# Last phase of a two-layer metaformer: two of eight normalisations and a bias move from ACT and DVE to POOL, and DVE adds the residual a slot later

## The reference, cut to what matters

```python
y = conv(dw3(dw2(dw1(x))), pw_w)          # 1x1 convolution after three depthwise ones
x = x + y * x_normed                      # gate
t = tokens(x)                             # [pixels, 96]
n = (t - mean(t)) / sqrt(var(t) + 1e-5)   # over the 96 channels
h = relu(q16(q16(q8(n) @ W1.T) + q8(b1)))
t = t + q16(q16(q8(h) @ W2.T) + q8(b2))
```

## Time and profile before

| | us |
|---|---|
| median of 3 runs | 3661.55 (3657.33 to 3664.26) |
| the profiled execution's own time | 3659.49 |
| its span | 3657.6 |
| phase C | from about 2500 to the end |

### The profile page before, as it was taken

One profiled execution on the slowest core, in us unless ns is written; L12 is line 12 of the kernel. 1 busy time (PEld: TensorE's weight loads), 2 busy tenths in 40 slices (PEclk: granted clock), 3 DMA queues, 4 the chain that ended last, 5 costly groups with the idle time before them and its releaser, 6 DMA issues. The chain is left out here.

```text
span 3657.6 us, 68122 instructions
## 1 busy us (share of the span) xinstructions
PE 3017.4 (82%) x21990; PEld 1910.0 (52%) x21990; DVE 3218.4 (88%) x8131; ACT 2781.3 (76%) x6274; POOL 1728.9 (47%) x2404
## 2 busy tenths in 40 slices
PE   6787888878787878887876799997888888888887
PEld 5565665656565656565654344443444444444444
DVE  4888889898989898989886699999899999999998
ACT  2577777777777877777778455554799999999998
POOL 3777777777787877787864000000222222222221
PEclk9999999899999999999987899999999999999999
DMA  3233323232323232323212888897676667666762
GB/s 68 53 89 74 91 71 88 71 88 70 88 71 88 71 88 71 88 71 88 71 56 69 212 238 234 236 280 212 172 199 188 181 185 200 184 184 193 199 177 83
DMA packets 696178, 478.92 MB, mean 131 GB/s; under 512 B 407217, under 2 KB 674422, under 8 KB 683830
## 3 DMA queue, kind: packets, MB, share of 16 engines
q1 hardware_dynamic: 695830, 474.58, 49.2%
HBM read 272.09 MB, written 201.92 MB: 130 GB/s over the span
## 5 line engine op out<-in xcount | busy, mean ns | idle before, releaser
L1891 POOL TENSOR_SCALAR C_var<-C_st 128x16 f32<-128x16 f32 x64 | 13.5, 211 | 1338.6 <-DVE C_st L178 1338.6
L1464 DVE SCALAR_TENSOR_TENSOR B_y<-B_mid,B_coefs,B_y 128x512 f32<-128x512 f32 x768 | 509.0, 750 | 3.2 <-ACT B_y L1429 3.2
L1395 PE MATMUL B_ps_row<-B_z,B_band 128*128 128x512 f32 x1152 | 499.1, 596 | 15.1 <-DMA B_band<-edge_scratch 15.1
L378 DVE TENSOR_SCALAR A_hq<-A_h,A_b 128x512 f16<-128x512 f16 x768 | 319.4, 456 | 176.5 <-ACT A_h L370 169.6
L370 ACT ACTIVATE A_h<-A_hid 128x512 f16<-128x512 f32 x768 | 428.3, 594 | 59.5 <-PE A_hid L357 57.1
L178 DVE BATCH_NORM_STATS2 A_st<-A_xT 128x6 f32<-128x192 f32 x1536 | 443.6, 349 | 29.3 <-ACT A_xT L861 16.0
L370 ACT ACTIVATE C_h<-C_hid 128x512 f16<-128x512 f32 x768 | 425.0, 589 | 22.9 <-PE C_hid L357 22.5
L1504 ACT ACTIVATE C_q<-C_xT,C_shift,C_rstd 128x96 fp8e5<-128x96 f32 x1024 | 392.6, 457 | 43.3 <-POOL C_shift L1898 43.2
L894 ACT ACTIVATE A_xc<-A_xT,A_shift,A_rstd 128x96 f32<-128x96 f32 x1024 | 379.3, 456 | 4.2 <-POOL A_shift L1207 4.0
L167 POOL TENSOR_TENSOR A_rstd<-A_var,A_expo 128x16 f32<-128x16 f32 x128 | 376.5, 2941 | 10.7
L1395 PEld LDWEIGHTS B_ps_row<-B_z,B_band 128*128 128x128 f32 x1152 | 218.8, 190 | 294.2 <-issue 287.8
(11 more groups left out here) (167 smaller groups left out, 7248.7 us busy)
## 6 DMA issues: line engine op xcount, KB each, us to landing
A_xq<-in_x SPq DMA_DIRECT2D x32, 1536.0 KB, 8.9
x_scratch<-A_xT SPq DMA_DIRECT2D x64, 768.0 KB, 3.2
x_scratch<-A_x3h SPq DMA_DIRECT2D x64, 768.0 KB, 5.4
B_z<-x_scratch SPq DMA_DIRECT2D x96, 512.0 KB
y_scratch<-B_y SPq DMA_DIRECT2D x96, 512.0 KB, 3.6
C_x3q<-x_scratch SPq DMA_DIRECT2D x32, 1536.0 KB, 9.1
C_xT<-x_scratch SPq DMA_DIRECT2D x64, 768.0 KB, 16.6
C_y3q<-y_scratch SPq DMA_DIRECT2D x31, 1536.0 KB, 15.6
```

Source lines behind the costliest of these rows:

```text
L378: r = dve.tensor_scalar(self.hq[:, b, s], self.h16[:, b, s], self.w["b1"][:, j:j + 1], 0.0, ALU.add, ALU.max)
L1395: m = pe.matmul(bank(c, h), band[c.buf(NB)][:, d, :], z[c.buf(NB)][:, half(h), d:d + W], start=(d == 0), stop=(d == 2))
L1464: dve.scalar_tensor_tensor(y, mid[c.buf(2)][:, half(h), t:t + W], coefs[:, c.n, 3 + t:4 + t], y, ALU.mult, ALU.add).then_inc(ev["sums"], 1)
```

## The change

- `LN_AT` loses groups 3 (slot 0) and 7 (slot 4). POOL normalises them in `pool_norm`, with two tensor operations per group: scale by the reciprocal deviation into a new float32 tile `scaled`, then add the shift into `q8`. New semaphores `normp` and `scaled` go with it. POOL does group 7 of a unit in its slot 1 and group 3 of the next unit in slot 5.
- `dve_y` becomes `pool_y`: the second layer's bias is added by POOL, for all 8 groups, in slots 1 to 8.
- DVE's `out` of group k moves from the end of slot k+1 to slot k+2, and there it stands behind `dve_hidden` and in front of `gate`. `out` of group 7 goes to slot 0 of the next step.

```diff
-LN_AT = {6: (1, 0), 7: (1, 1), 8: (1, 2), 0: (0, 3), 1: (0, 4), 2: (0, 5), 3: (0, 6), 4: (0, 7)}
+LN_AT = {6: (1, 0), 7: (1, 1), 8: (1, 2), 1: (0, 4), 2: (0, 5), 3: (0, 6)}
+POOL_GROUP = 3
...
+    def pool_norm(self, pool, i, k):
+        ev, t = self.ev, slice(k * TPC, (k + 1) * TPC)
+
+        pool.wait_ge(ev["ln2"], ev.at("ln2", i, k // 4))
...
+        x = self.x_of(i)[:, k * CW:(k + 1) * CW].rearrange("p (t c) -> p t c", c=C)
+        pool.tensor_tensor(self.scaled[:], x, per_token(self.rstd[:, t], TPC), ALU.mult).then_inc(ev["scaled"], 1)
+        pool.wait_ge(ev["scaled"], ev.at("scaled", i, k // 4))
+        pool.tensor_tensor(self.q8[:, t, :], self.scaled[:], per_token(self.shift[:, t], TPC), ALU.add,
+                           saturate=False).then_inc(ev["normp"], 1)
...
-    def dve_y(self, dve, i, k):
+    def pool_y(self, pool, i, k):
         ev = self.ev
 
-        dve.wait_ge(ev["y16"], ev.at("y16", i, k))
-        dve.tensor_scalar(self.y16b[:, k % 2, :], self.y16[:, k % 2, :], self.w["b2"][:, 0:1], None,
-                          ALU.add).then_inc(ev["yb"], 1)
+        pool.wait_ge(ev["y16"], ev.at("y16", i, k))
+
+        if k >= 2:
+            pool.wait_ge(ev["out"], ev.at("out", i, k - 2))
...
+        pool.tensor_scalar(self.y16b[:, k % 2, :], self.y16[:, k % 2, :], self.w["b2"][:, 0:1], None,
+                           ALU.add).then_inc(ev["yb"], 1)
...
             def body(i):
-                q = i + 1
+                q, p = i + 1, i - 1
                 for s in range(FFN_SLOTS):
                     if i.real and s < NK:
                         ff.dve_hidden(dve, i, s)
+                    if s == 0 and p.real:
+                        out(p, NK - 1)
+                    if i.real and s >= 2:
+                        out(i, s - 2)
                     if q.real and s < NK:
                         gate(q, s)
                     if q.real and s >= 1:
                         x4(q, s - 1)
-                    if i.real and s >= 1:
-                        ff.dve_y(dve, i, s - 1)
                     if q.real and s >= 1:
                         stats(q, s - 1)
-                    if i.real and s >= 1:
-                        out(i, s - 1)
...
             def body(i):
                 q = i + 1
-                for half in range(2):
-                    if q.real:
-                        norm_terms(q, half)
+                for s in range(1, FFN_SLOTS):
+                    if i.real:
+                        ff.pool_y(pool, i, s - 1)
+                    if i.real and s == 1:
+                        ff.pool_norm(pool, i, 4 + POOL_GROUP)
+                    if q.real and s % 4 == 0:
+                        norm_terms(q, s // 4 - 1)
+                    if q.real and s == 5:
+                        ff.pool_norm(pool, q, POOL_GROUP)
```

More of the change, by code:

```diff
@@ L1494, in __init__, with normed @@
         self.shift = sb("shift2", [P, NT], F32)
+        self.scaled = sb("scaled", [P, TPC, C], F32)
+    def normed(self, i, k):
+        if k % 4 == POOL_GROUP:
+            return self.ev["normp"], self.ev.at("normp", i, k // 4)
+        return self.ev["norm2"], self.ev.at("norm2", i, k - k // 4)
+    def pool_norm(self, pool, i, k):
+        ev, t = self.ev, slice(k * TPC, (k + 1) * TPC)
+        pool.wait_ge(ev["ln2"], ev.at("ln2", i, k // 4))
+        earlier = i if k // 4 else i - 1
+        if begun(earlier):
+            pool.wait_ge(ev["normp"], ev.at("normp", earlier, 1 - k // 4))
+        if begun(i - 1):
+            pool.wait_ge(ev["q8_full"], ev.at("q8_full", i - 1, k))
+        x = self.x_of(i)[:, k * CW:(k + 1) * CW].rearrange("p (t c) -> p t c", c=C)
[3 more added lines that the diff above has]
+                           saturate=False).then_inc(ev["normp"], 1)
     def act_norm(self, act, i, k):
@@ L1509, in pe_q8 @@
         ev, ring = self.ev, self.ring
-        pe.wait_ge(ev["norm2"], ev.at("norm2", i, k))
+        pe.wait_ge(*self.normed(i, k))
         name, unit, pos = ring.before(step, "q8", k)
@@ L1546, in act_y @@
         act.activation(self.y16[:, k % 2, :], self.ring.bank("y", k)[0:C, 0:CH], ACT.Copy).then_inc(ev["y16"], 1)
-    def dve_y(self, dve, i, k):
+    def pool_y(self, pool, i, k):
         ev = self.ev
-        dve.wait_ge(ev["y16"], ev.at("y16", i, k))
-        dve.tensor_scalar(self.y16b[:, k % 2, :], self.y16[:, k % 2, :], self.w["b2"][:, 0:1], None,
-                          ALU.add).then_inc(ev["yb"], 1)
+        pool.wait_ge(ev["y16"], ev.at("y16", i, k))
+        if k >= 2:
+            pool.wait_ge(ev["out"], ev.at("out", i, k - 2))
+        elif begun(i - 1):
+            pool.wait_ge(ev["out"], ev.at("out", i - 1, NK - 2 + k))
+        pool.tensor_scalar(self.y16b[:, k % 2, :], self.y16[:, k % 2, :], self.w["b2"][:, 0:1], None,
+                           ALU.add).then_inc(ev["yb"], 1)
 class LastBuffers:
@@ L1632, in phase_c @@
                 back_uses += [("y", s - 1, 0, "y16", s - 1), ("c", s - 1, 0, "out", s - 1)]
-        ev = Events(nc, ctx, "C_", dict(x1=NK, bn2=NK, ln2=2, ln2_s=6, norm2=NK, q8_full=NK, y_full=NK, c_full=NK, q8c=NK,
+        ev = Events(nc, ctx, "C_", dict(x1=NK, bn2=NK, ln2=2, ln2_s=6, norm2=NK - 2, normp=2, scaled=2, q8_full=NK, y_full=NK, c_full=NK, q8c=NK,
                                         hidden=NJ * NK, h16=NJ * NK, relu=NK, hq=NK, y16=NK, yb=NK, out=NK, pw_full=NK,
@@ L1862, in body @@
                         x4(q, s - 1)
-                    if i.real and s >= 1:
-                        ff.dve_y(dve, i, s - 1)
                     if q.real and s >= 1:
                         stats(q, s - 1)
-                    if i.real and s >= 1:
-                        out(i, s - 1)
             steps(dve, body)
+            out(Unit(0, NQ - 1, 4, NQ - 1), NK - 1)
         @block.gpsimd
@@ L1882, in norm_terms @@
                 if begun(q - 1):
-                    pool.wait_ge(ev["norm2"], ev.at("norm2", q - 1, 4 * half + 3))
+                    pool.wait_ge(*ff.normed(q - 1, 4 * half + 2))
                     pool.sem_inc(ev.passed, 1)
+                    pool.wait_ge(*ff.normed(q - 1, 4 * half + 3))
                 earlier = q if half else q - 1
```

## The result

The changed kernel takes 3840.9 us (median of 4 runs, 3831.0 to 3843.8) against 3662.2: a ratio of 1.0485, with a 95% interval of 1.0463 to 1.0507. It is slower, as forecast, but by 179 us where 78 were forecast, and outside the range (3680 to 3795). The profiled execution took 3839.9 us with a span of 3838.1. All of it is in phase C, whose unit went from 33.5 to 39.3 us (31 times 5.7 is 178 us): gate 7 of the first unit stands at 2578.0 us in both profiles.

The account below looks back on a forecast made before the run. ACT and DVE, both nearly full, were taken to bound phase C; with out, the ring would. 1.5 (ring) - 0.1 (gate 7 to gate 2) + 1.2 (collisions) = 2.6 us a unit, 31 repeats, 81 us: 3740 us, range 3680 to 3795.

Parts of the forecast that it names:

- the ring: Gate through mix, hid2, h2, third 378 and rounding to next gate: 4.17 us with out, +1.5 us a unit.
- gate 7 to gate 2: Stretch where POOL's terms for groups 4 to 7 are the chain: 13.87 against 13.99 us, -0.1 us a unit.
- the collisions: POOL's normalisations hold up DVE's 378s and rounding: 0.5 in slot 2, 0.7 in slot 6, 1.2 us a unit.
- That it moves out into the ring: In slots 2 to 7 out, 0.59 us, now stands between rounding and gate, lengthening the gate-to-gate path from 3.58 to 4.17.
- PE's transpose of q8 ... pushes mix by an estimated 0.05: For groups 4 to 7 the transpose waits for out and delays mix by 0.05 us in four slots.
- The 0.7 us of a bias addition: Estimated length of POOL's 96x512 addition, taken between 0.26 and 0.85 us; eight make 5.6 us a unit.
- The bias additions themselves mostly fall beside x4 and the statistics: POOL's bias additions run beside DVE work that is not held up, so they add no collision time.
- DVE, and later ACT, would idle: DVE idles about 0.5 us a slot before the third 378; ACT idles before h2 in each slot, ended by PE.
- Faster: Rival: out hides and ACT's and DVE's own work sets slots 2 to 7, 1 us a unit less: 3628 us, chance 0.15.
- Collisions in every slot: Rival: each bias addition also stops a 378 or rounding, 0.25 in eight slots, 2 us a unit more: 3802 us, chance 0.1.

Follow-up runs that it names:

- out alone: Against the kernel before, only DVE's out moves a slot later, in front of gate; bias stays on DVE, all groups on ACT: 3721.3 us, ratio 1.0168.
- Out behind gate: Changed kernel with out of the same slot put right behind gate instead of in front of it: 3872.8 us, ratio 1.0585.
- out + bias: Changed kernel with all eight groups normalised on ACT again; POOL keeps the bias additions, out stays moved: 3747.3 us, ratio 1.0243.
- changed + fill: Changed kernel with PE given extra work: the c_turn transposes of groups 1 and 5 are issued four times, same output: 3797.8 us, ratio 1.0379.
- Norms alone: Against the kernel before, only the normalisations of groups 3 and 7 go to POOL; bias and out as before: 3726.2 us, ratio 1.0187.
- norms at chosen places: Kernel before with groups 3 and 7 normalised on POOL, held until DVE turns to PSUM; bias on DVE, out unmoved: 3674.5 us, ratio 1.0038.

## Why the prediction was wrong where it was

The forecast was 2.6 us a unit, and 5.74 were measured. By its own terms: the ring, 1.5 from gate 2 to gate 7, was nearly right (1.73 in "out alone"); gate 7 to gate 2, -0.1, is +1.8; the collisions, 1.2, are 3.0 by length, though not all of it on the path; and the clock, for which there was no term, is 1.4. The last three overlap.

- **Direction and first cause: right.** "That it moves out into the ring" is shown by "out alone": +1.84 us a unit, 63 us, with POOL untouched. I had +1.4 (1.5 - 0.1).
- **Which ring: the step that was mis-sized by a little.** "PE's transpose of q8 ... pushes mix by an estimated 0.05". It pushes ACT, not mix: ACT's copy of q8 stands before h0, h1 and h2, and that ring is 4.27, not 4.17. "Out behind gate" shows it as the bound (4.87 = 4.27 + 0.60).
- **The 0.7 us of a bias addition: wrong.** It is 1.56 at least, outside the bounds of 0.26 and 0.85, which I took from other forms. The Trainium skill (GPSIMD Engine Reference, section 4.1, Engine selection) calls GPSIMD roughly line-rate for operations with one input and about 2x slower than VectorE for those with two. Here the operation with one input is the longer: 1.5 to 1.6 us with one tensor, 1.09 with two, at the same 96x512. The measurement decides. With it POOL's queue slips, and slot 6 gets a block of 3.5 us. "The bias additions themselves mostly fall beside x4 and the statistics" fails with it: in "out + bias" they make the 378s and roundings 1.3 us a unit longer. Making the addition 0.5 us shorter gave back 34 us.
- **"-0.1 us" from gate 7 to gate 2: wrong.** By the table it is 15.83 for 14.02, +1.8. With only norms or only the bias on POOL besides `out` it is 14.42 and 14.46, so it takes both. In the unit shown `norm_terms` begins 4.70 and not 3.75 us after gate 7, and the 378s and the rounding of slot 2 take 1.5 us longer, where I had 0.5 for group 7. Some 0.5 of the 1.8 is clock (15.32 in "changed + fill").
- **"1.2 us a unit" of collisions: short.** Norms alone cost 1.92 against before, though they take 2.88 us off ACT. In slot 6 the group costs 0.85 (5.12 - 4.27, bias on DVE), and 1.28 (5.55 - 4.27) with the bias addition in front of it, not 0.7. That it is a matter of place is shown by "norms at chosen places": 68 us down to 15.
- **No term for the clock: the step that was missing.** I wrote that DVE, and later ACT, would idle, and never asked what PE's longer waits do. It waits 1.8 and 2.3 us in slots 3 and 7, and the clock falls after them; "PE kept busy" gives 43 us, a quarter of the loss.
- **Worth of the rivals.** "Faster" was wrong; the ring is closed through a bank that it did not consider either. "Collisions in every slot" came nearest (3802) for the wrong reason: slot 5 of the changed kernel has none and slot 4 only 0.1 us.

The loss by its parts, per unit of 39.29 - 33.55 = 5.74 us: the ring 1.84; norms on top of it 1.42 (36.81 - 35.39, part of it clock); the bias on top of both 2.48 (39.29 - 36.81); of the whole, 1.41 is the clock (39.29 - 37.88). The parts do not add in another order, since the bias alone on top of the ring costs 0.83.

## What to carry to other kernels

Before an instruction is moved on a busy engine, follow each bank and buffer that it frees: a ring is closed by whoever waits for the bank, and here that wait came out through ACT. Work given to an idle POOL is not free because POOL is idle; ask which of DVE's instructions run beside it: the same two normalisations cost 68 us where they met lines 378, and about 15 at a chosen place, where they met x4, the statistics and one of DVE's bias additions each. And where a change makes waits, ask what they do to TensorE's clock: the clock that fell behind two waits of about 2 us in each unit cost 43 us here.

## What the runs showed of the hardware

- POOL's addition of a scalar to 96x512 took 1.51 us (constant) to 1.60 us (per partition, half or single precision); as an addition of two tensors, 1.09 us. Why is open; that it is not the type, and that the pointer makes only 0.09 us of it, is shown.
- Three of DVE's instructions whose operands all lie in SBUF, and POOL's tensor operations and bias additions, held each other up: line 378 up to 1.06 us for 0.35, line 382 up to 1.14 for 0.56, DVE's bias addition 0.98 for 0.34 (norms placed), POOL's second operation up to 1.02 for 0.83. DVE's instructions with a PSUM operand (0.68), and the statistics (0.35 each), ran beside them at their own length.
- In the changed kernel the granted clock fell to its lower level 40 times in 27 units, nearly always behind PE's waits in slots 3 and 7 (1.8 and 2.3 us on average). In "out alone", whose PE waits 1.14 us at most, it did not fall, and with more PE work in the same slots it fell once.
